# Two graph-attention layers on one core: layer 1's scores as three float32r products of rounded parts and remainders, its adjacency in five tiles in turn, and a new order of TensorE's items

## The reference, cut to what matters

```python
h = relu(layernorm(x));  x = x + layer0(h, adj)      # scores + beta*adj, masked where adj <= 0
h = relu(layernorm(x));  x = x + layer1(h, adj, adj)

def layer1(x, spatial, edge):                        # both are adj here
    q, k, v = x @ Wq.T, x @ Wk.T, x @ Wv.T + bv      # split in 12 heads of 32
    scores = q @ k.T * 384**-0.5 + (spatial + edge)
    row_nonzero = any(scores != 0, axis=-1)          # a row of zeros gives zero output
    p = nan_to_num(softmax(where(row_nonzero, scores, -inf)))
    return (p @ v) @ Wo.T + bo
```

## Time and profile before

| what | us |
|---|---|
| median of 3 runs (1963.05 to 1965.38) | 1964.48 |
| the profiled execution, its time | 1964.66 |
| its span, first to last instruction | 1962.9 |
| PE busy | 1893.7 (96%) |
| DVE busy | 1823.9 (93%) |
| ACT busy | 1609.8 (82%) |
| POOL busy | 994.5 (51%) |

### The profile page before, as it was taken

One profiled execution on the slowest core, in us unless ns is written; L12 is line 12 of the kernel. 1 busy time (PEld: TensorE's weight loads), 2 busy tenths in 40 slices (PEclk: granted clock), 3 DMA queues, 4 the chain that ended last, 5 costly groups with the idle time before them and its releaser, 6 DMA issues.

```text
span 1962.9 us, 50025 instructions
## 1 busy us (share of the span) xinstructions
PE 1893.7 (96%) x18336; PEld 1227.4 (63%) x18336; DVE 1823.9 (93%) x3989; ACT 1609.8 (82%) x4151; POOL 994.5 (51%) x1237
## 2 busy tenths in 40 slices
PE   5999999999999999997999999999999999999999
PEld 4666666666666666665666666666666666666665
DVE  6999999999999999998899999999999999999994
ACT  6899888998998889987887777877787777877785
POOL 6466655556667555564353444344343444344331
PEclk9999999999999999998999999999999999999999
DMA  4888899989899999897887887887787887787774
GB/s 156 201 216 227 222 232 232 236 231 240 223 232 224 231 228 237 228 242 204 210 229 189 220 201 201 208 211 198 201 210 191 218 202 209 198 209 202 201 194 128
DMA packets 105074, 415.91 MB, mean 212 GB/s; under 512 B 27104, under 2 KB 31200, under 8 KB 104832
## 3 DMA queue, kind: packets, MB, share of 16 engines
q1 hardware_dynamic: 78352, 306.29, 64.8%
q0 software_dynamic: 26480, 106.44, 17.2%
HBM read 88.61 MB, written 25.17 MB: 58 GB/s over the span
## 4 chain that ended last, share of the span: by engine, by line
PE 64%; DVE 30%; issue 3%; ACT 1%; POOL 1%; DMA 1%; SPq 0%; DVEq 0%; POOLq 0%
DVE s L428 16%; PE ring L302 15%; PE sc L267 15%; PE out L363 11%; DVE pt L441 11%; PE ring L284 6%; PE ring L331 6%; PE ring L310 5%; PE ring L293 2%; PE ring L333 1%; PE ring L322 1%; DVE stats L487 1%; DVE nmax L428 1%; ACT s L550 1%; DMA room<-in_wq 0%
## 5 line engine op out<-in xcount | busy, mean ns | idle before, releaser
L550 ACT ACTIVATE s<-s,nmax 128x512 f32<-128x512 f32 x1536 | 1096.0, 728 | 200.2 <-DVE nmax L428 198.8
L428 DVE CUSTOM_DVE_ANT_0 s<-sc,bias 128x512 f32<-128x512 f32 x1536 | 968.1, 686 | 57.1 <-PE sc L267 36.5
L441 DVE STREAM_TRANSPOSE pt<-s 128x2048 f32<-128x2048 f32 x285 | 656.9, 2305 | 0.0
L267 PE MATMUL sc<-k,q 32*128 32x512 f32 x3072 | 439.9, 642 | 49.9 <-DVE nmax L428 42.7
L550 ACT ACTIVATION_READ_ACCUMULATOR s<-s,nmax 128x1 f32 x1536 | 313.3, 204 | 0.0
L363 PE MATMUL out<-pk,v 128*32 128x192 f32 x6080 | 286.5, 329 | 0.0
L363 PEld LDWEIGHTS out<-pk,v 128*32 128x32 f32 x6080 | 178.0, 109 | 135.5 <-issue 98.2
L724 POOL TENSOR_TENSOR v<-v,bvx 128x384 f32<-128x384 f32 x64 | 64.6, 1009 | 369.9 <-ACT v L612 369.9
L310 PE MATMUL ring<-wv,hT 128*128 128x384 f32 x1152 | 247.7, 352 | 0.0
L302 PE MATMUL ring<-hT,wq 128*128 128x512 f32 x864 | 243.3, 414 | 1.5 <-DVE hT L456 1.5
L302 PE MATMUL ring<-hT,wk 128*128 128x512 f32 x864 | 239.7, 416 | 0.0
(11 more groups left out here) (94 smaller groups left out, 1896.9 us busy)
## 6 DMA issues: line engine op xcount, KB each, us to landing
pk<-pt SPq DMA_DIRECT2D x1520, 192.0 KB, 4.5
bias<-in_adj POOLq DMA_DIRECT2D x31, 1024.0 KB, 9.3
res<-in_x POOLq DMA_DIRECT2D x16, 768.0 KB, 4.9
x_between<-res POOLq DMA_DIRECT2D x16, 768.0 KB, 5.4
xin<-x_between POOLq DMA_DIRECT2D x16, 768.0 KB, 6.9
res<-x_between POOLq DMA_DIRECT2D x16, 768.0 KB, 5.3
xin<-in_x POOLq DMA_DIRECT2D x15, 768.0 KB, 8.5
out_x<-res POOLq DMA_DIRECT2D x15, 768.0 KB, 3.8
```

The source lines that it names most:

```text
L267: mm = nc.tensor.matmul(m.sc[:, j, :], m.q[rows, s % 2, P * t:P * (t + 1)], m.k[rows, s % 2, :], start=True, stop=True)
L428: nc.vector.tensor_tensor_reduce(out=m.s[:, t % 2, j, :], in0=m.sc[:, j, :], in1=m.bias[g % 2][:, t, :], scale=s_scale[layer], scalar=3.0e ...
L441: nc.vector.transpose(out=to, in_=m.s[:, t % 2].rearrange("p j (i a e) -> p (j i) a e", a=QUADS, e=HD)).then_inc(turned, 1)
L550: nc.scalar.activation(tile, tile, ACT.Exp, bias=m.nmax[s % 2][:, t, j:j + 1], scale=-1.0, accum_out=m.sums[s % 2][:, t, j:j + 1]).then_in ...
```

## The change

1. In layer 1, GpSimd copies q and k of each chunk into float32r (`q_high`, `k_high`: rounded) and subtracts that from the full value, in place (`q_low`, `k_low`: remainder). The scores are three float32r products, high x high, high x low and low x high, one after the other into the same bank: twelve matmuls of 32 rows in place of eight instructions. The scores of a chunk, and `sums`, now wait for `split_done`.
2. `sums` multiplies the sums of k with both parts of q, still as float32: twice the matmuls.
3. Layer 1's adjacency lies in five tiles that are used in turn, over the space of the two old buffers; each tile has a DMA of 256 KB (`load_tile`, steps 4, 10, 9, 12), and its buffer is free when its old tile's last scores are read.
4. Row sums of the adjacency: ScalarE, one activation with accumulation per tile (`sum_adj`), in place of six additions on GpSimd and a reduction on VectorE.
5. Layer 1's `PLACES` are new; the two pieces of each q, k and v result mostly come next to each other. `X_STEP`, `ADJ_STEP`, `RES_STEP` and `BIAS_STEPS` change, the last also for layer 0.
6. The new tiles lie in one arena; layer 1's weights are staged in the upper part of the first adjacency buffer, and layer 1's bias of v is loaded after layer 0's last mask.

```diff
+SLOTS = NT + 1
+PRODUCTS = ((0, 0), (0, 1), (1, 0))
+SPLIT_LAYERS = (1,)
...
-    "hT": (-4.50, -4.41, -4.30),
-    "qk_first": (-2.92, -1.93, 1.05, 2.07, 4.69, 6.07),
-    "qk": (-2.75, -1.82, 1.25, 2.42, 5.12, 6.10),
-    "v_first": (-3.45, -0.53, 0.74, 3.46),
-    "v": (-3.40, -0.07, 1.20, 3.82),
-    "sums": (0.30, 4.30, 9.76),
-    "zero": (2.09, 5.92, 10.64),
-    "tp": (3.31, 3.32, 3.33, 3.34, 7.31, 7.32, 7.33, 7.34, 11.31, 11.32, 11.33, 11.34),
-    "pv": (6.31, 7.28, 8.12, 9.31, 10.69, 12.12, 13.86, 14.69, 16.12),
-    "spread": (7.30, 11.62, 14.21),
-    "post": (17.30, 17.58, 18.08, 20.41),
+    "hT": (-4.314, -4.31, -4.306),
+    "qk_first": (-2.914, -2.428, 0.803, 1.023, 4.399, 5.701),
+    "qk": (-2.713, -2.427, 0.804, 1.024, 4.4, 5.802),
+    "v_first": (-3.146, -0.967, 0.808, 2.229),
+    "v": (-3.145, -0.966, 1.009, 2.23),
+    "sums": (0.7, 3, 9.956),
+    "zero": (2.729, 6.814, 10.336),
+    "tp": (3.01, 3.02, 3.03, 3.04, 7.11, 7.12, 7.13, 7.14, 11.66, 11.67, 11.68, 11.69),
+    "pv": (6.495, 6.824, 8.12, 9.96, 10.736, 10.924, 14.398, 14.99, 16.62),
+    "spread": (5.984, 10.32, 14.394),
+    "post": (17.1, 17.58, 18.78, 18.81),
...
-X_STEP, ADJ_STEP, RES_STEP, BIAS_STEPS = 9, (1, 5), (6, 3), (3, 5, 6, 8)
+X_STEP, ADJ_STEP, RES_STEP, BIAS_STEPS = 8, 0, (6, 1), (1, 2, 7, 10)
+TILE_STEPS, SUM_STEPS = (4, 10, 9, 12), (9, 12, 13, 14)
...
                     if (g, c) == (B - 2, 2):
+                        sp.wait_ge(bias_done, NT * B)
+                        load_row(m.bvx, bv[1], bv_in[1])
+                        sp.wait_ge(scores_done, UNITS * DT * (B - 1))
                         load_weight(1, 2)
...
+                if t == 0 and split:
+                    pe.wait_ge(split_done, nth_split(s, 1))
...
+                qs, ks = ((m.q_high, m.q_low), (m.k_high, m.k_low)) if split else ((m.q,), (m.k,))
+                products = PRODUCTS if split else PRODUCTS[0:1]
+                for n, (a, b) in enumerate(products):
+                    for j in range(HC):
+                        rows = slice(HD * j, HD * (j + 1))
+                        mm = nc.tensor.matmul(m.sc[:, j, :], qs[a][rows, s % 2, P * t:P * (t + 1)], ks[b][rows, s % 2, :],
+                                              start=n == 0, stop=n == len(products) - 1)
...
                     pe.wait_ge(ksum_done, nth("sums", g, i))
+                    pe.wait_ge(split_done, nth_split(DT * g + i, 0))
+                    for part in (m.q_high, m.q_low):
+                        for t in range(NT):
+                            mm = nc.tensor.matmul(to[HD * t:HD * (t + 1), 0:P], m.ksum[:, at, :], part[:, at, P * t:P * (t + 1)].bitcast(F32),
+                                                  start=part is m.q_high, stop=part is m.q_low)
...
+            def sum_adj(g, i):
+                b = g - B
+                act.wait_ge(tile_loaded[i], LOADS * (b + 1))
...
+                nc.scalar.activation(m.unused[:], adj_tile(g, i), ACT.Copy, accum_out=m.biassum[g % 2][:, i, :]).then_inc(adj_summed, 1)
...
+            def load_tile(g, t):
+                n = NT * (g - B) + t
+                if n == 0:
+                    pool.wait_ge(scores_done, UNITS * DT * (B - 1))
+                if 0 < n < NT:
+                    pool.wait_ge(weights_split[1], 2)
+                if n == SLOTS - 1:
+                    pool.wait_ge(scores_done, UNITS * DT * B)
+                if n >= SLOTS:
+                    old, tile = B + (n - SLOTS) // NT, (n - SLOTS) % NT
+                    pool.wait_ge(scores_done, UNITS * (DT * old + DT - 1) + HC * (tile + 1))
+                pool.dma_start(adj_tile(g, t), tokens(adj[g % B])[:, t]).then_inc(tile_loaded[t], 16)
+
+            def split(g, a, i):
+
+                s = DT * g + a
+                full, high, low = ((m.q, m.q_high, m.q_low), (m.k, m.k_high, m.k_low))[i]
+                pool.wait_ge(done["qk"], nth("qk", g, 2 * a + i))
+                nc.gpsimd.tensor_copy(high[:, s % 2, :], full[:, s % 2, :]).then_inc(split_high, 1)
+                pool.wait_ge(split_high, nth_split(s, i))
+                nc.gpsimd.tensor_tensor(low[:, s % 2, :], full[:, s % 2, :], high[:, s % 2, :].bitcast(F32), ALU.subtract).then_inc(split_done, 1)
...
                 for x in step_before(g, c, t):
+                    if x[0] == "qk" and layer_of(x[1]) in SPLIT_LAYERS:
+                        split(x[1], x[2] // 2, x[2] % 2)
...
-                    if layer_of(g + 1) and (c, t) == (2, 2):
-                        sum_bias(g + 1)
```

More of the change, by code:

```diff
@@ L187, in graph_at, with adj_tile, nth_split @@
             return n // (NT * DT) if n % (NT * DT) == 0 and 0 < n // (NT * DT) < GRAPHS else None
+        def adj_tile(g, t):
+            return m.adj[:, (NT * (g - B) + t) % SLOTS, :] if layer_of(g) else m.bias[g % 2][:, t, :]
+        def nth_split(s, i):
+            return 2 * (s - DT * B * SPLIT_LAYERS[0]) + i + 1
         def steps():
@@ L397, in _ @@
                         first_shares((x[2] % HC,))
+            last_part = ("pv", GRAPHS - 1, PARTS * (DT - 1) - 1)
+            if last_part not in CLOSING:
+                first_shares((2, 3))
             for x in CLOSING:
@@ L427, in scores @@
                 for j in range(HC):
-                    nc.vector.tensor_tensor_reduce(out=m.s[:, t % 2, j, :], in0=m.sc[:, j, :], in1=m.bias[g % 2][:, t, :],
+                    nc.vector.tensor_tensor_reduce(out=m.s[:, t % 2, j, :], in0=m.sc[:, j, :], in1=adj_tile(g, t),
                                                    scale=s_scale[layer], scalar=3.0e38, op0=ALU.add, op1=ALU.min,
@@ L654, in _ @@
                     item(*x)
+                for ahead in range(max(g, B), min(g + 2, GRAPHS)):
+                    for i in range(NT):
+                        if number(g, c, t) == NT * DT * (ahead - 1) + (max(SUM_STEPS[i], NT * DT) if ahead == B else SUM_STEPS[i]):
+                            sum_adj(ahead, i)
                 if (g, c, t) in ROUNDINGS:
@@ L825, in _ @@
                 for x in step_before(g, c, t):
+                    if x[0] == "qk" and layer_of(x[1]) in SPLIT_LAYERS:
+                        split(x[1], x[2] // 2, x[2] % 2)
+                for ahead in range(max(g, B), min(g + 2, GRAPHS)):
+                    for i in range(NT):
+                        if number(g, c, t) == NT * DT * (ahead - 1) + TILE_STEPS[i]:
+                            load_tile(ahead, i)
+                for x in step_before(g, c, t):
                     if x[0] == "v":
@@ L828, in _ @@
                 if g + 1 < GRAPHS:
-                    if at == ADJ_STEP[layer]:
-                        if layer == 0:
-                            pool.wait_ge(bias_done, NT * (g + 1))
+                    if at == ADJ_STEP and layer_of(g + 1) == 0:
+                        pool.wait_ge(bias_done, NT * (g + 1))
                         if g:
@@ L886, in __init__ @@
         self.hT = [sb(f"hT{i}", [P, DT, N], F32R) for i in range(2)]
-        self.q, self.k = sb("q", [P, 2, N]), sb("k", [P, 2, N])
         self.v = sb("v", [P, 2, NT, D])
-        self.bias = [sb(f"bias{i}", [P, NT, N]) for i in range(2)]
-        self.biassum, room = sb("biassum", [P, NT, 1]), sb("room", [P, 2 * N + NT * N // 8])
-        self.part = room[:, 0:N].rearrange("p (h n) -> p h n", h=2)
-        self.rwide = room[:, N:2 * N].rearrange("p (t n) -> p t n", t=NT)
-        self.eighth = room[:, 2 * N:2 * N + NT * N // 8].rearrange("p (t n) -> p t n", t=NT)
-        self.mask = sb("mask", [P, N])
-        self.rspread = self.mask
+        self.biassum = [sb(f"biassum{i}", [P, NT, 1]) for i in range(2)]
         self.s = sb("s", [P, 2, HC, N])
@@ L907, in __init__, with at @@
         self.ksum1, self.ksum = sb("ksum1", [P, 2]), sb("ksum", [P, 2, HD])
-        self.headsum = sb("headsum", [P, P])
         self.oT = sb("oT", [P, DT, N])
         self.onorm = self.wo
+        arena = nc.sbuf_base
+        sb("arena", [P, ARENA])
+        def at(name, first, shape, dt=F32):
+            return nc.alloc_sbuf_tensor_at(name, shape, dt, offset=arena + 4 * first)
+        tiles, pair = 2 * NT * N, 2 * N
+        self.bias = [at(f"bias{i}", i * NT * N, [P, NT, N]) for i in range(2)]
+        self.q_high, self.k_high = at("q_high", tiles, [P, 2, N], F32R), at("k_high", tiles + pair, [P, 2, N], F32R)
+        self.q, self.k = at("q", tiles + 2 * pair, [P, 2, N]), at("k", tiles + 3 * pair, [P, 2, N])
+        self.q_low, self.k_low = at("q_low", tiles + 2 * pair, [P, 2, N], F32R), at("k_low", tiles + 3 * pair, [P, 2, N], F32R)
+        rest = tiles + 4 * pair
+        self.mask = at("mask", rest, [P, N])
+        self.adj = at("adj", 0, [P, SLOTS, N])
+        staged = at("staged", NT * N - DT * D, [P, DT, D])
+        for n in range(3):
+            self.raw[1][n] = staged[:]
+        self.rspread, self.rwide = at("rspread", SLOTS * N, [P, N]), at("rwide", (SLOTS + 1) * N, [P, NT, P])
+        self.unused = at("unused", (SLOTS + 2) * N, [P, N])
```

(1 more changed line is left out.)

68 lines of the change are left out of this document (26 added, 42 removed).

## The result

The changed kernel takes a median of 2069.98 us (four runs, 2064.45 to 2077.20), the kernel before, on the same chip, 1963.76: a ratio of 1.0537, with an interval of 1.0519 to 1.0555. It is slower by 106 us, where 1954.5 was forecast, 10 us less than the 1964.48 that the prediction started from. The profiled execution took 2064.45 us.

What follows compares the result with a forecast made beforehand. TensorE was taken to bound layer 1, VectorE layer 0. Net -0.88 us a pass times 16 gives -14.1; with +3 at the border and +1 in layer 0, -10.1, so 1954.5 us, range 1936 to 1981.

Steps and rivals of the forecast that it cites:

- What goes beside other work: Row sums on ScalarE, halvings on GpSimd, SP's moves and tile loads: covered by idle time; new waits and loads 0.
- Scores, sums: TensorE, layer 1: scores from 1.07 to 0.89 us a step, saving 2.16 a pass; `sums` adding 0.68 a pass.
- Rival 3: TensorE scores, layer 1: float32r streams no faster than float32 in 32-row form, scores 1.50 us; 2063, chance 0.03.
- Rival 2: TensorE scores, layer 1: products wait for their weight loads, scores 1.11 us; 1993, chance 0.08.
- Rival 1: GpSimd, layer 1: halves of q and k come late, TensorE waits about 1 us a pass; 1970, chance 0.12.
- Rivals 4 and 5: TensorE, layer 1. First: waits eat the gain, 1962, chance 0.15. Second: all of it arrives, 1937, chance 0.12.
- Regrouping and new waits: TensorE, layer 1: +0.1 us a pass for changes to 32-column groups, +0.5 for waits on VectorE in iterations 1 and 3.
- Border of the layers: Once, between layers: graph 16's k asked for one iteration earlier while its weights arrive as late; +3 us (0 to 5).
- Layer 0: GpSimd's queue: two masks ahead of v's last bias delay `pv` about 0.4 us, mostly hidden; +1 us in all (0 to 8).

Runs made afterwards that it cites:

- e1: Changed kernel with only `pv5` back from place 10.924 to its old 12.12: 1975.86 us, ratio 1.0054.
- e4: e1 with layer 0's steps for loads and masks as before the change: 1963.70 us, ratio 0.9987.
- f1: e4 with layer 1's scores as one float32 product and `sums` from the full q: 1984.58 us, ratio 1.0119.
- e3: Changed kernel, `pv5` still early, with layer 1's input load, result store and third adjacency tile issued at later steps: 1994.35 us, ratio 1.0143.
- f4: e4 with only layer 0's masks at the changed kernel's steps 1, 2, 7, 10: 1977.50 us, ratio 1.0067.
- f2: e4 with TensorE's items dealt more evenly, layer 1's input load at step 9 and third adjacency tile at 10: 1959.82 us, ratio 0.9978.
- f5: f2 with the last `pv` of a graph at place 16.1: 1963.67 us, ratio 0.9992.
- f6: f5 with `pv5` at place 11.99, the end of iteration 11: 1970.48 us, ratio 1.0029.
- g1: Kernel before the change with `pv5` early at 10.9 and layer 1's input load at step 8 in place of 9: 1985.97 us, ratio 1.0107.
- f3: f2 with layer 1's scores as one float32 product and `sums` from the full q: 1971.96 us, ratio 1.0042.

## Why the prediction was wrong

**The step that failed** is the end of "What goes beside other work": "The four tile loads move the same megabyte, each issued at least two steps before its first reader; 0", and beside it that SP's new waits have "only the next chunk's moves behind them. Both: 0". It looked at when the loads' own readers want them, and not at what the loads run beside. No sentence looked at the input's load and the result's store, which `X_STEP` and the place of `post3` moved, or set `pv5`, moved from 12.12 to 10.924, against the landing of its blocks. With the table above it could have been set: 8.7 us spare before, 7.2 of which the new place takes (64.4 to 57.2), and 1.8 MB put in front of the moves. The runs showed a wait of some 5 us a pass in place of the 0, 71.6 us in all, and with what hangs on it 94 us (the change less e1). Part of that is PE's clock: behind the stall `pv5` takes 2.79 us for 1.51.

**Scores, sums**: right. 0.90 us for 0.89 reckoned, and `sums` hold PE for 0.46 (1271.83 to 1272.29) where they held it for 0.33 in the earlier trace rows, so +0.13 for 0.23 reckoned; e4's iteration 3, where transposes follow, has 0.57 for the predicted 0.56. e4 against f1 gives -1.35 us a pass, or -1.16 by the median, for the forecast -2.16 + 0.68 = -1.48.

**Rival 3** had the time, 2063, by an accident of sums: scores at 1.50 us were its mechanism, and they take 0.90. **Rival 2** falls by the loads of one step's scores in PEld's timeline, which answer to the earlier trace rows:

```profile
1262.27 0.19 PEld L287 LDWEIGHTS sc<-k_high,q_high 32*128 32x128 f32 x4 [0.17 <-DVE nmax L455]
1262.38 0.20 PEld L287 LDWEIGHTS sc<-k_low,q_high 32*128 32x128 f32 x4
1262.62 0.19 PEld L287 LDWEIGHTS sc<-k_high,q_low 32*128 32x128 f32 x4
```

Each product's weights come in while the product before runs (1262.38 in 1262.28 to 1262.61, 1262.62 in 1262.61 to 1262.84), in the same rows. The rule of the Trainium skill that the rival went by ("TensorE: Matmul & The Clock Gate", Part 3, The mechanism) does not fit these rows. **Rival 1** did not come: the copy takes 0.61 us, below the bound of 0.67, the subtraction 1.29, and no matmul of the changed kernel waits for either. (In e4 nine weight loads of the steady passes wait 1.1 us for a remainder, but VectorE's read holds the matmuls behind them longer.) **Rivals 4 and 5** never had their case, since the stall covers both; without it, in e4 and in pass 30, the waits eat the gain (0.9987; 63.34 us), much as rival 4 had it. ScalarE's busy time in a pass rose from 49.23 us to 50.55 and GpSimd's from 26.63 to 33.91; none of PE's waits in layer 1's steady passes is put down to either, as reckoned, though a delay by way of VectorE is not excluded.

**Regrouping and new waits**, +0.6 us a pass: mis-sized, and this alone would have taken most of the gain. In pass 30 PE is busy for 61.87 us, 1.01 less than in the earlier trace rows where 1.38 was reckoned, and idle for 1.47 against 0.45, so 1.0 more where 0.5 was reckoned: together the pass is back at 63.34. In e3, whose order is the change's, the pass less its wait for blocks is 64.45 - 1.3 = 63.1, where the prediction's terms give 62.44; the uneven iterations 1 and 3 were the right ones, 4.60 and 4.01 us for 3.9 and 3.4 reckoned with 0.4 of waiting each: 0.7 and 0.6. That is some 10 us over the run, 12 by pass 30 without its 0.18.

**Border of the layers**, +3: wrong in sign. Passes 15 and 16 take 126.44 us together in e4, 129.57 before, so -3.1. The +2.5 that the changed kernel shows there (132.02) comes with the stall in it.

**Layer 0**, +1 with a bound of 8: 12 to 14 us in e4 and f4. The hold of the first mask was carried over from the earlier trace rows at 3.78 us, but the load does not come earlier by as much as the masks do: their waits add up to 161.7 us in the changed kernel, 51.8 before, and the longest is 12.6.

The parts as measured: products -21, the rest of the change +20 (f1 against before), layer 0 +12, the stall +94, together +105. Each is the difference of two neighbours in one chain of kernels from before to the change, so that the sum comes out says nothing on its own; what stands behind each part is its own experiment.

Not settled: which of store and tile does most, since neither was tried alone (pass 30 shows only that the two without the load, and the store earlier, do no harm); why SP's issues stretch; and what bounds f2's pass at 62.9 us, since f5 and f6 tried only two other places.

## What to carry to other kernels

When an item is moved ahead in one engine's order, write down when each of its inputs lands, the small DMAs included, and what of that margin the new place leaves. When a large transfer is moved, look not only at its own reader but at which small, urgent transfers it will run beside, in the windows where the DMA share is already 1. A mean share of 0.8 over a pass does not show such a window.

## What was not expected of the hardware

SP's issue instruction is not of fixed length. It takes 0.59 us in the median, 0.63 with one GpSimd load beside the moves (g1), and 1.10 in the median with 2.80 as the longest where load, store and tile run beside them. TensorE, idle for 5.19 us, came back at a granted clock of 0.50, and ran 4.4 us of work at it, so the stall cost more than its length. And the time that three products save depends on the deal: 1.16 us a pass in one order and 0.92 in the other, by the median pass (e4 against f1, f2 against f3).
